# A megakernel on one core: the latents of seven batches move from a stage of their own into the attention stage that reads them

## The chip, the core and the metric

The kernel runs on 1 core of one Trainium2 chip as a single program. The metric is the device time in microseconds: the median of the runs. One execution was taken by the hardware profiler, and every row below is from that execution. Engines: PE is TensorE (PEld its weight loads), DVE is VectorE, ACT is ScalarE, POOL is GpSimd, SP is SyncE, which here only issues transfers.

## What is computed

Two layers on `x` of 8 batches x 512 tokens x 512 columns and a context of 8 batches x 77 tokens x 512. Layer 0 is a cross-attention and a routed slot block; layer 1 is a perceiver attention, whose queries, called latents here, come from the normalised token stream, and a choice of one expert out of 8 per token. The part around the change:

```python
# layer 0's last step, per batch (64 slots):   x2 = x1 + alpha @ vo + bo
x  = x + out                          # out = (alpha @ slot_values) @ wo + bo
# layer 1:
xn = layernorm(ctx_1024, ln_x_g, ln_x_b)            # 8 x 77 x 512
ln = layernorm(_layernorm(x), ln_l_g, ln_l_b)       # 8 x 512 x 512: the latents z
q  = ln @ Wq                                        # 16 heads of 64
k, v = split(concatenate((xn, ln), axis=1) @ Wkv)   # 77 + 512 keys
attn = softmax(where(mask, q k^T, -max))
out  = layernorm((attn @ v) @ Wout, ln_o_g, ln_o_b)
x    = x + out                                      # then the experts
```

All products are in float32: a tensor is kept as a high part in a rounded format and a low part (what the rounding left), and a product takes three matmuls (high x high, low x high, high x low; `product`, the records of L119 to L121).

## The kernel before, in words

The program runs in stages, one after the other, each a function with one instruction list per engine; all engines meet between stages. `build_slots` (L999) makes the slot values, `build_latents` (L1325) all latents and the context's keys and values, `build_perceiver` (L1661) the attention, `build_experts` (L2135) the rest. `two_layers` (L2836) calls them in this order.

**Latents stage.** SP loads the context rows at the start of the stage, and the token rows x1 of batch 2 and after into a ring of three buffers; x1 of batches 0 and 1 was loaded by the slots stage (L1099). For batch b, TensorE runs `read_out(b+1)` (four products alpha x vo with a row of ones for the bias, L1478), `transposed(b)` (16 transposes, L1486), `keys(b)` (24 matmuls of 308 columns for a pair of heads of all batches' context) and one or two `values` items (12 matmuls of 512 columns). VectorE runs `add_and_measure(b)` (adds the product to x1, L1608; statistics, L1611; aggregate, L1616), then the normalise (L1631), the low parts of the latents (L1641), of the keys (L1646) and of the values (L1651). GpSimd raises the variance to the power -1/2. ScalarE applies gain and bias (L1556), makes the high parts (L1560, L1574, L1582) and stores the latents' low part. The context's own path at the start: statistics (L1594), normalise (L1623), transposes (L1495, L1500), gain and bias (L1537), high (L1546) and low parts (L1638). Two banks serve keys and values; the value tile `Vst` is single, and ScalarE waits for its store (`V_out`) before it fills it for the next chunk (L1582, store L1423).

**Perceiver.** 128 heads of 4 ticks each; a tick n is 128 queries of one head against 589 keys, and each engine goes through the ticks in a loop written by hand, so the order of its work is fixed. TensorE in tick n issues the scores of tick n+1 (L1942, L1944), and, by n mod 8 (a pair of heads), transposes of the probabilities (L1955), the weighted sums (L1971, L1972) and the queries, keys and values of the next pair. The transposes, queries, keys and values share three banks `W`; `claim` takes the one released longest ago and waits for its readers. VectorE in tick n: reciprocal of the row sums (L2109), minimum over the scores (L2113), reads of the `W` banks (low parts `PTl`, keys `U`, values, all L2066), the addition of the output (L2098). ScalarE: exponential (L2034), high parts of the same banks (L2005), the copy and the high part of the output (L2053). GpSimd: probabilities times the reciprocal (L1880), and the output's low part (`low_part`, L1874), one per pair at tick 2 of a head. SP loads the latents of a batch (`load`, L1770), the keys, and stores the outputs (`store`). At the start GpSimd clears `Ql`, `Um` and the tails of `U`, 20 signals in all, and TensorE waits for all of them ahead of its first product:

```python
pe.wait_ge(setup, 20)
for n in range(1 - LEAD, STEPS + 2 * NT + 1):
    g, t = divmod(n, NT)
```

Of the kernel before, what the change touches and what calls it, by code (L numbers as in the profile page):

```python
# [20 lines left out]
P = 128  # L21
# [977 lines left out]
def build_slots(nc, orders, a, si_s, vo_s, Wq, Wkv, Wout_s, gh_s, WihT, x1_s):  # L999
# [11 lines left out]
    with ExitStack() as ctx:  # L1011
# [71 lines left out]
        def _(sp):  # L1083
# [15 lines left out]
            for n in range(2):  # L1099
                sp.dma_start(stage(n), x1_s[n:n + 1].rearrange("b (t p) d -> p (b t) d", p=P)).then_inc(x1_in, 16)  # L1100
# [5 lines left out]
            sp.wait_ge(x1_in, 32)  # L1106
# [218 lines left out]
def build_latents(nc, orders, a, x1_s, alphaT_s, vo_s, x2_s, z_s, Kc_s, Vc_s, Wkv, ahead):  # L1325
# [13 lines left out]
    RING = 3  # L1339

    with ExitStack() as ctx:
# [18 lines left out]
        rows_c = [f32(z_hi[1][:, k, :]) for k in range(KT - 1)] + [f32(z_lo[1][0:LAST, 0, :])]  # L1360
# [3 lines left out]
        setup, small, ones_row, cx_in = sem("setup"), sem("small"), sem("ones_row"), sem("cx_in")  # L1364
        x1_in = [sem(f"x1_in{r}") for r in range(RING)]
# [10 lines left out]
        batch = lambda b: 0 <= b < B  # L1376
        v_items = [(k, h) for k in range(KT) for h in range(2)]
        v_of = lambda b: v_items[b * len(v_items) // B:(b + 1) * len(v_items) // B]
        place = {"x2": lambda b, t: (b * NT + t) % 3, "zT": lambda b, c: 3 + (b * C + c) % 3, "cT": lambda c: 3 + c % 3,
# [20 lines left out]
        def _(sp):  # L1400
            flat = a["ctx_1024"].rearrange("b s d -> (b s) d")
            def load_small(b):
                m = b % 2
                if b >= 2:
                    sp.wait_ge(*pe_s.after("x2", b - 2, NT - 1))
# [3 lines left out]
            def load_x(b):  # L1409
                r = b % RING  # L1410
                if b >= RING:
                    sp.wait_ge(x2_out[r], 16 * (b // RING))
                    sp.wait_ge(*dve_s.after("xn", b - RING, NT - 1))
                sp.dma_start(X[r], x1_s[b:b + 1].rearrange("b (t p) d -> p (b t) d", p=P)).then_inc(x1_in[r], 16)
# [12 lines left out]
            for k in range(KT):  # L1427
                sp.dma_start(rows_c[k], flat[k * P:k * P + rows_of(k), :]).then_inc(cx_in, 16)
            for dst, src in smalls:
                sp.dma_start(dst, src).then_inc(small, 16)  # L1430
            load_small(1)
            load_x(2)
            for b in range(B):
                sp.wait_ge(*dve_s.after("free", "x2", b, NT - 1))
                sp.dma_start(x2_s[b:b + 1].rearrange("b (t p) d -> p (b t) d", p=P), X[b % RING]).then_inc(x2_out[b % RING], 16)
                if batch(b + 2):
                    load_small(b + 2)
                if batch(b - 1):
                    for q, h in [i for i in v_of(b - 1) if i[1]]:
                        values_out(q)  # L1440
                    keys_out(b - 1)
                if batch(b + 2) and b > 0:
                    load_x(b + 2)
            for q, h in [i for i in v_of(B - 1) if i[1]]:
                values_out(q)
            keys_out(B - 1)
            for r in range(RING):
                sp.wait_ge(x2_out[r], 16 * len(range(r, B, RING)))
# [5 lines left out]
        def _(pool):  # L1454
# [8 lines left out]
            for b in range(B):  # L1463
# [7 lines left out]
        def _(pe):  # L1471
# [52 lines left out]
            for b in range(B):  # L1524
                if batch(b + 1):
                    read_out(b + 1)
                transposed(b)
                keys(b)
                for k, h in v_of(b):
                    values(k, h)  # L1530

        @block.scalar
        def _(act):
# [14 lines left out]
            def latents(b):  # L1548
                m = b % 2
                if b >= 2:  # L1550
                    act.wait_ge(z_out[m], 32 * (b // 2))
                for c in range(C):
                    act.wait_ge(*pe_s.after("zT", b, c))
                    if b >= 2:
                        act.wait_ge(*dve_s.after("lo", b - 2, C - 1))
# [12 lines left out]
            for b in range(B):  # L1568
                latents(b)
# [6 lines left out]
                low_out(b)  # L1576
# [6 lines left out]
            for m in range(2):  # L1583
                act.wait_ge(z_out[m], 32 * (B // 2))

        @block.vector
        def _(dve):
# [3 lines left out]
            for k in range(KT):  # L1591
                r = rows_of(k)
                dve.wait_ge(cx_in, 16 * KT)
# [7 lines left out]
            def add_and_measure(b):  # L1601
                r, m = b % RING, b % 2
                dve.wait_ge(*dve_s.after("c var"))
                if b >= 2:
                    dve.wait_ge(x1_in[r], 16 * (b // RING + (r == 2)))
# [7 lines left out]
                if b >= 2:  # L1613
                    dve.wait_ge(*pool_s.after("ve", b - 2))
# [4 lines left out]
            add_and_measure(0)  # L1619
# [4 lines left out]
            for b in range(B):  # L1624
                r, m = b % RING, b % 2
                dve.wait_ge(*pool_s.after("rstd", b))
                dve.wait_ge(*dve_s.after("var", b))
                if b >= 1:
                    dve.wait_ge(*pe_s.after("zT", b - 1, C - 1))
# [3 lines left out]
                if batch(b + 1):  # L1633
                    add_and_measure(b + 1)
                if b == 0:
                    for c in range(C):
                        dve.wait_ge(*act_s.after("zc hi", c))
                        dve.tensor_tensor(zc[1][:, c, :], zc_full[c][:, :], f32(zc[0][:, c, :]), ALU.subtract).then_inc(*dve_s.mark("zc", c))  # L1638
                for c in range(C):
                    dve.wait_ge(*act_s.after("hi", b, c))  # L1640
                    dve.tensor_tensor(z_lo[m][:, c, :], full[m][:, c, :], f32(z_hi[m][:, c, :]), ALU.subtract).then_inc(*dve_s.mark("lo", b, c))  # L1641
# [19 lines left out]
def build_perceiver(nc, orders, a, z_s, Kc_s, Vc_s, o_s, xs_s, mask_s, Wq, Wkv, Wout_s):  # L1661
# [25 lines left out]
    with ExitStack() as ctx:  # L1687
# [315 lines left out]
        def _(act):  # L2003
# [26 lines left out]
            for n in range(1 - LEAD, STEPS + 2 * NT + 1):  # L2030
# [25 lines left out]
                if t == 3:  # L2056
                    probabilities(g - 1, 4)
# [848 lines left out]
```

## Time and profile before

| what | us |
|---|---|
| median of 3 runs (2,917.95 to 2,927.77) | 2,923.05 |
| the profiled execution | 2,921.61 |
| its span | 2,919.8 |
| latents stage, from the trace | 828.5 to 999.7 |

A row of a timeline reads: start, duration, engine, line and operation, output<-inputs, partitions x elements, and in brackets the idle time of the engine just before it with what ended it. A row with xN groups N instructions in a row. In the page's groups the columns are busy time, mean ns of one, idle before and its releaser. In the windows the columns are the stretch, its length, the busy time of PE, PEld, DVE, ACT and POOL, then PEclk, the mean clock granted to TensorE as a share of full speed, the busy share of the DMA engines and GB/s. In the waits: the waiting engine and line, whom it waited for, us in total, times, the longest.

### The profile page before, as it was taken

The numbers are of one execution on the slowest core, as the hardware profiler recorded it, in microseconds if no ns is written. First come the engines' busy times: TensorE is split into PE (matmuls) and PEld (weight loads), VectorE is DVE, ScalarE is ACT, GpSimd is POOL, SyncE is SP. The second block draws the span as 40 slices with busy tenths as digits, with TensorE's granted clock in tenths as the row PEclk, the third lists the DMA queues.
The fourth block names the chain that finished last, engine by engine and source line by source line (L and its number), as shares of the span: only waits on it lengthen the run. The fifth ranks groups of instructions, "written<-read, shape, count | busy, mean of one in ns | idle before, by whom it ended". The sixth has DMA issues, their size and how long they took to land. (4 is left out here: it accounts for less than half of the span.)

```text
span 2919.8 us, 41005 instructions
## 1 busy us (share of the span) xinstructions
PE 2646.1 (91%) x14566; PEld 2188.7 (75%) x14566; DVE 2023.6 (69%) x4005; ACT 1517.6 (52%) x2897; POOL 1522.0 (52%) x1149
## 2 busy tenths in 40 slices
PE   6699999986778699999999999999999998799698
PEld 5577777763436588888888888888888887677476
DVE  3677777742546377777777777777777777577666
ACT  2234334331213277777777777777777777111175
POOL 2355544320000166666666666666666666465555
PEclk9899999998878899999999999999999999899899
DMA  5212222133348633334333343233433314668475
GB/s 188 56 54 56 56 57 57 41 96 128 139 145 312 228 74 80 106 83 115 81 77 109 80 118 81 75 111 76 122 80 77 109 51 136 210 238 288 157 275 187
DMA packets 212526, 351.15 MB, mean 120 GB/s; under 512 B 75839, under 2 KB 82370, under 8 KB 204631
## 3 DMA queue, kind: packets, MB, share of 16 engines
q1 hardware_dynamic: 193539, 284.89, 32.8%
q0 software_dynamic: 11680, 45.02, 4.2%
q10 hardware_dynamic: 7104, 18.61, 1.6%
q8 instruction: 117, 1.92, 0.3%
q14 instruction: 86, 0.70, 0.1%
HBM read 172.47 MB, written 156.64 MB: 113 GB/s over the span
## 5 line engine op out<-in xcount | busy, mean ns | idle before, releaser
L1880 POOL TENSOR_SCALAR pa_Pr<-pa_Pr,pa_rs 128x590 f32<-128x590 f32 x512 | 902.4, 1769 | 485.1 <-DVE pa_rs L2109 484.9
L2113 DVE TENSOR_REDUCE pa_least<-pa_S 128x1 f32<-128x590 f32 x512 | 390.7, 763 | 230.0 <-PE pa_S L1944 227.9
L2034 ACT ACTIVATE pa_Pr<-pa_S,pa_least 128x590 f32<-128x590 f32 x512 | 385.5, 753 | 99.4 <-DVE pa_least L2113 96.0
L2066 DVE TENSOR_TENSOR pa_PTl<-pa_W,pa_PTh 128x512 fp32r<-128x512 f32 (+1 forms) x640 | 421.2, 684 | 20.5 <-ACT pa_PTh L2005 16.4
L2005 ACT ACTIVATE pa_PTh<-pa_W 128x512 fp32r<-128x512 f32 (+1 forms) x640 | 367.0, 596 | 58.4 <-PE pa_W L1955 47.1
L1955 PE MATMUL pa_W<-pa_ident,pa_Pr 128*128 128x128 f32 (+1 forms) x2560 | 369.7, 275 | 0.6
L1955 PEld LDWEIGHTS pa_W<-pa_ident,pa_Pr 128*128 128x128 f32 (+1 forms) x2560 | 302.4, 142 | 30.0 <-POOL pa_Pr L1880 2.8
L1971 PE MATMUL pa_O<-pa_PTh,pa_V 128*128 128x512 f32 (+1 forms) x640 | 289.2, 452 | 18.6 <-DVE pa_PTl L2066 14.4
L1972 PE MATMUL pa_O<-pa_PTl,pa_V 128*128 128x512 f32 (+1 forms) x640 | 253.4, 396 | 0.0
L1942 PE MATMUL pa_S<-pa_U,pa_Qh 128*128 128x296 f32 (+1 forms) x1024 | 228.9, 305 | 7.5 <-ACT pa_Pr L2034 0.5
L1942 PEld LDWEIGHTS pa_S<-pa_U,pa_Qh 128*128 128x128 f32 x1024 | 183.2, 188 | 55.5 <-ACT pa_Pr L2034 21.3
L1944 PE MATMUL pa_S<-pa_Um,pa_Ql 128*128 128x296 f32 (+1 forms) x1024 | 222.7, 299 | 0.0
L514 POOL TENSOR_TENSOR l_E<-l_E,l_rs 128x1232 f32<-128x1232 f32 x32 | 81.1, 2533 | 204.0 <-DVE l_rs L916 204.0
L1944 PEld LDWEIGHTS pa_S<-pa_Um,pa_Ql 128*128 128x128 f32 x1024 | 166.4, 189 | 0.0
L1971 PEld LDWEIGHTS pa_O<-pa_PTh,pa_V 128*128 128x128 f32 (+1 forms) x640 | 121.4, 190 | 45.0 <-DVE pa_PTl L2066 36.1
L119 PE MATMUL pa_W<-Wkv_hi,pa_z_hi 128*128 128x256 f32 x512 | 144.9, 283 | 0.0
L120 PE MATMUL pa_W<-Wkv_lo,pa_z_hi 128*128 128x256 f32 x512 | 144.2, 282 | 0.0
L121 PE MATMUL pa_W<-Wkv_hi,pa_z_lo 128*128 128x256 f32 x512 | 143.9, 281 | 0.0
L1972 PEld LDWEIGHTS pa_O<-pa_PTl,pa_V 128*128 128x128 f32 (+1 forms) x640 | 123.0, 192 | 5.2
L2560 ACT ACTIVATE ex_xT_hi<-ex_bank 128x512 fp32r<-128x512 f32 x92 | 53.4, 599 | 141.3 <-PE ex_bank L2456 134.9
L119 PE MATMUL pa_W<-pa_z_hi,Wq_hi 128*128 128x512 f32 x256 | 106.9, 418 | 17.8 <-POOL pa_Ql L1871 17.8
L2005 ACT ACTIVATE pa_U<-pa_W 64x512 fp32r<-64x512 f32 x128 | 75.8, 592 | 89.7 <-PE pa_W L121 88.1
(503 smaller groups left out, 6545.6 us busy)
## 6 DMA issues: line engine op xcount, KB each, us to landing
xs_s<-pa_Ql SPq DMA_DIRECT2D x57, 576.0 KB
pa_Um<-pa_U SPq DMA_DIRECT2D x128, 147.5 KB
pa_Qh<-pa_Qh SPq DMA_DIRECT2D x128, 128.0 KB
o_s<-pa_O_hi SPq DMA_DIRECT2D x64, 256.0 KB, 2.0
o_s<-pa_O_lo SPq DMA_DIRECT2D x64, 256.0 KB, 2.3
Wkv_hi<-o_s SPq DMA_DIRECT2D x8, 2048.0 KB, 11.3
Wkv_lo<-o_s SPq DMA_DIRECT2D x8, 2048.0 KB, 17.0
l_xa<-x SPq DMA_DIRECT2D x8, 1024.0 KB, 6.5
```

What stands on the lines that cost most here:

```text
L119: pe.matmul(out, a[0], b[0], start=first, stop=False)
L120: pe.matmul(out, a[0], b[1], start=False, stop=False)
L1880: pool.tensor_scalar(p, p, rs[:, g % 2, t:t + 1], None, ALU.mult).then_inc(*pool_s.mark("probs", n))
L1942: pe.matmul(out[:, a0:a1], qh, U[p % 2][x][:, a0:a1], start=True, stop=False)
L1944: m = pe.matmul(out[:, a0:a1], ql, Um[p % 2][x][:, a0:a1], start=False, stop=True)
L1955: m = pe.transpose(bank_of[u][0:KEYS[c], t * P:(t + 1) * P], Pr[g % 2][:, t, c * P:c * P + KEYS[c]], ident[:, :])
L1971: pe.matmul(Oc[:, :], v, PTh[0:n, r, :], start=(c == 0), stop=False)
L1972: pe.matmul(Oc[:, :], v, PTl[0:n, r, :], start=False, stop=(c == NC - 1)).then_inc(*pe_s.mark("PV", g, c))
L2005: act.activation(out, src, ACT.Copy, scale=scale).then_inc(*act_s.mark("hi", *name))
L2034: act.activation(Pr[g % 2][:, t, :], scored[n % 2], ACT.Exp, scale=-1.0, bias=least[:, g % 2, t:t + 1], accum_out=rs[:, g % 2, t:t + 1]).t ...
L2066: dve.tensor_tensor(out, src, f32(hi_ap), ALU.subtract).then_inc(*dve_s.mark(*name))
L2113: dve.tensor_reduce(least[:, g % 2, t:t + 1], scored[n % 2], AX, ALU.min).then_inc(*dve_s.mark("least", n))
```

## The change

Four things change together.

1. The latents stage keeps batch 0 only (`RING, FIRST = 1, 1`), and its order is turned: the context goes first, its rows now loaded by the slots stage in place of x1 of batch 1; then come keys and values for all eight pairs of heads, with batch 0's latents after the first round. Keys are stored ahead of values.
2. The latents of batches 1 to 7 are made in the perceiver as 28 tiles of 128 rows, one every 12 ticks (`APART`), each spread over ticks -2 to 8 from its beginning: fetch, row of ones, residual product, add and statistics, store of x2, power, normalise, transposes, gain and bias, high part, low part, and the stores of both. The two new TensorE steps claim `W` banks. SP's load of a batch waits for the stores of its latents.
3. To make room the output's low part overwrites its sum: ScalarE's copy of the next output waits for the store (`o_out`) instead of for the low part. The high part comes at tick 1 of a head, not at tick 2, and so does the low part.
4. At the start VectorE clears `Um` and the tails of `U` (8 signals, `blanks_done`), GpSimd only `Ql`; TensorE waits for both at its first scores instead of ahead of its first product.

The diff, cut to its core:

```diff
@@ build_slots, SP
-            for n in range(2):
-                sp.dma_start(stage(n), x1_s[n:n + 1].rearrange("b (t p) d -> p (b t) d", p=P)).then_inc(x1_in, 16)
+            sp.dma_start(stage(0), x1_s[0:1].rearrange("b (t p) d -> p (b t) d", p=P)).then_inc(x1_in, 16)
+            flat = a["ctx_1024"].rearrange("b s d -> (b s) d")
+            whole = flat.shape[0] // P
+            sp.dma_start(stage(1)[:, 0:whole, :], flat[0:whole * P, :].rearrange("(k p) d -> p k d", p=P)).then_inc(x1_in, 16)
+            sp.dma_start(stage(2)[0:flat.shape[0] - whole * P, 0, :], flat[whole * P:, :]).then_inc(x1_in, 16)
@@ build_latents
-    RING = 3
+    RING, FIRST = 1, 1
...
+            for b in range(PAIRS):
+                keys_out(b)
+                for q, h in [i for i in v_of(b) if i[1]]:
+                    values_out(q)
...
-            read_out(0)
-            context()
-            for b in range(B):
-                if batch(b + 1):
-                    read_out(b + 1)
-                transposed(b)
+            context()
...
+            for b in range(FIRST):
+                read_out(b)
+            for b in range(PAIRS):
                 keys(b)
                 for k, h in v_of(b):
                     values(k, h)
+                if batch(b):
+                    transposed(b)
@@ build_perceiver
+        APART = 3 * NT
+        tiles = [(b, t) for b in range(1, B) for t in range(NT)]
+        begins = {STEPS // B * (b - 1) + APART * t: i for i, (b, t) in enumerate(tiles)}
+        tile_at = lambda n, late: begins.get(n - late)
@@ SP
             def load(b):
+                if b:
+                    sp.wait_ge(z_out, 32 * NT * b)
...
+                if p == 0:
+                    sp.wait_ge(blanks_done, 8)
@@ GpSimd
-                    pool.memset(f32(Um[m][x][:, :]), 0.0).then_inc(setup, 1)
-            for m in range(2):
-                for x in range(2):
-                    pool.memset(f32(U[m][x][:, T + SK:Z]), 0.0).then_inc(setup, 1)
...
-                if t == 2 and g >= 3 and g % 2 == 1:
+                if t == 1 and g >= 3 and g % 2 == 1:
                     low_part((g - 3) // 2)
+                i = tile_at(n, 2)
+                if i is not None:
+                    pool.wait_ge(*dve_s.after("x2 var", i))
+                    pool.tensor_scalar(lve, lmv[:, 1:2], 1.0 + EPS, EPS * EPS, ALU.mult, ALU.add).then_inc(*pool_s.mark("x2 ve", i))
+                    pool.wait_ge(*pool_s.after("x2 ve", i))
+                    pool.tensor_tensor(lrstd, lve, minus_half, ALU.pow).then_inc(*pool_s.mark("x2 rstd", i))
@@ TensorE
             def scores(n):
...
+                if n == 0:
+                    pe.wait_ge(setup, 13)
+                    pe.wait_ge(blanks_done, 8)
...
-            pe.wait_ge(setup, 20)
+            def residual(i):
+                u = ("x2", i)
+                claim(u)
+                pe.wait_ge(x_in, 32 * (i + 1))
+                pe.wait_ge(vo_in, 16 * (i // NT + 2))
+                pe.wait_ge(*dve_s.after("ones", i))
+                pe.matmul(bank_of[u][:, :], alphas[0:NS + 1, :], vo[:, :], start=True, stop=True).then_inc(*pe_s.mark(*u))
+                release(u)
+            def latent(i):
+                u = ("zT", i)
+                claim(u)
+                pe.wait_ge(*dve_s.after("xn", i))
+                for c in range(C):
+                    m = pe.transpose(bank_of[u][:, c * P:(c + 1) * P], ln[:, c * P:(c + 1) * P], ident[:, :])
+                m.then_inc(*pe_s.mark(*u))
+                release(u)
...
+                if tile_at(n, 0) is not None:
+                    residual(tile_at(n, 0))
+                if tile_at(n, 4) is not None:
+                    latent(tile_at(n, 4))
@@ ScalarE: fetch at tick -2, x2 store at 2, high part at 6, its store at 7, the low part's store at 8
+                    act.wait_ge(x2_out, 16 * (i + 1))
+                    act.wait_ge(*dve_s.after("read", "zT", i))
+                    act.activation(l_hi, ln[:, :], ACT.Copy).then_inc(*act_s.mark("z hi", i))
...
-                        act.wait_ge(*pool_s.after("O lo", p - 1))
+                        act.wait_ge(o_out, 32 * p)
                     copy(O[x * HD:(x + 1) * HD, :], Oc[(1 - x) * HD:(2 - x) * HD, :], "low", g - 2)
@@ VectorE
-            dve.wait_ge(setup, 20)
+            for m in range(2):
+                for x in range(2):
+                    dve.memset(f32(Um[m][x][:, :]), 0.0).then_inc(blanks_done, 1)
+                    dve.memset(f32(U[m][x][:, T + SK:Z]), 0.0).then_inc(blanks_done, 1)
+            dve.wait_ge(setup, 13)
...
+            def add_and_measure(i):
+                dve.wait_ge(*pe_s.after("x2", i))
+                dve.tensor_tensor(lx[:, :], bank_of["x2", i][:, :], lx[:, :], ALU.add).then_inc(*dve_s.mark("read", "x2", i))
...
+            def scaled(i):
...
+                for c in range(C):
+                    m = dve.tensor_scalar(ln[:, c * P:(c + 1) * P], bank_of["zT", i][:, c * P:(c + 1) * P], gain[0][:, c:c + 1], gain[1][:, c:c + 1],
+                                          ALU.mult, ALU.add)
...
+            def latent_low(i):
+                dve.wait_ge(*act_s.after("z hi", i))
+                dve.tensor_tensor(ln[:, :], ln[:, :], lx[:, :], ALU.subtract).then_inc(*dve_s.mark("z lo", i))
...
+                for late, work in ((-1, ones), (1, add_and_measure), (3, normalised), (5, scaled), (7, latent_low)):
+                    if tile_at(n, late) is not None:
+                        work(tile_at(n, late))
```

## Rows read from the trace of the kernel before

**Rows 1.** Windows of three stretches: the latents stage, its rounds, the perceiver.

```profile
828.50:999.70 171.20, 124.57 (x524) 90.96 (x524) 100.09 (x207) 59.45 (x102) 14.05 (x22) 0.82 0.72 263
...
862.00:990.00 128.00, 106.69 (x472) 81.00 (x470) 78.75 (x160) 48.31 (x84) 9.38 (x13) 0.88 0.80 300
...
1100.00:2400.00 1300.00, 1282.70 (x7962) 1128.05 (x7961) 1006.24 (x1877) 942.43 (x1933) 873.43 (x513) 1.00 0.34 91
```

**Rows 2.** Waits of VectorE, weight loads and GpSimd in the perceiver, 1100 to 2400.

```profile
DVE pa_least L2113 <- PE pa_S L1944: 207.5, 177, 1.8
...
PEld pa_O L1971 <- DVE pa_PTl L2066: 24.9, 64, 1.2
...
POOL pa_Pr L1880 <- DVE pa_rs L2109: 429.4, 285, 3.1
```

**Rows 3.** Timeline of the latents stage, TensorE.

```profile
853.73 3.62 PE L1478 MATMUL la_bank<-la_vo,la_aT 65*128 65x512 f32 x8
...
861.60 0.41 PE L119 MATMUL la_bank<-la_zc_hi,Wkv_hi 128*128 128x308 f32 x1 [2.13 <-DVE la_zc_lo L1638]
...
894.55 0.39 PE L119 MATMUL la_bank<-la_zc_hi,Wkv_hi 128*128 128x308 f32 x1
...
899.62 0.50 PE L119 MATMUL la_bank<-Wkv_hi,la_zc_hi 128*128 128x512 f32 x1 [1.42 <-DVE la_K_lo L1646]
...
902.53 2.74 PE L1478 MATMUL la_bank<-la_vo,la_aT 65*128 65x512 f32 x6
```

**Rows 4.** Timeline of the latents stage, the context's path, VectorE and ScalarE.

```profile
836.86 2.47 DVE L1594 BATCH_NORM_STATS2 la_cstats<-la_z_hi 128x6 f32<-128x512 f32 x4 [7.11 <-DMA la_z_lo<-ctx]
...
848.42 1.88 DVE L1623 TENSOR_SCALAR la_z_hi<-la_z_hi,la_cmv,la_crstd 128x512 f32<-128x512 f32 x4
...
855.56 1.32 ACT L1546 ACTIVATE la_zc_hi<-la_K_hi 128x616 fp32r<-128x616 f32 x2
```

**Rows 5.** Timeline: a value store on SP's queue, and ScalarE's next fill.

```profile
919.91 0.34 SPq L1423 DMA_DIRECT2D Vc_s<-la_V  x1
...
923.91 0.60 ACT L1582 ACTIVATE la_V<-la_bank 128x512 fp32r<-128x512 f32 x1 [4.75 <-PE la_bank L1478]
```

**Rows 6.** Timeline of the change of stages, SP's queue and TensorE.

```profile
991.02 0.32 SPq L1423 DMA_DIRECT2D Vc_s<-la_V  x1
...
1000.38 0.42 SPq L1770 DMA_DIRECT2D pa_z_lo<-z_s  x1
...
1007.42 0.79 PE L119 MATMUL pa_W<-pa_z_hi,Wq_hi 128*128 128x512 f32 x1 [17.79 <-POOL pa_Ql L1871]
```

**Rows 7.** DMA issues, 985 to 1020: KB each, median us to landing.

```profile
pa_z_lo<-z_s SPq DMA_DIRECT2D x1, 1024.0 KB, 6.9
```

**Rows 8.** Timeline of a pair of heads in the perceiver, VectorE and TensorE.

```profile
1783.54 0.77 DVE L2113 TENSOR_REDUCE pa_least<-pa_S 128x1 f32<-128x590 f32 x1 [1.75 <-PE pa_S L1944]
...
1787.39 1.28 DVE L2066 TENSOR_TENSOR pa_PTl<-pa_W,pa_PTh 128x512 fp32r<-128x512 f32 x2
...
1788.13 0.66 PE L1955 MATMUL pa_W<-pa_ident,pa_Pr 128*128 128x128 f32 x4
1788.54 0.48 PE L1971 MATMUL pa_O<-pa_PTh,pa_V 128*128 128x512 f32 x1
```

**Rows 9.** Groups of the latents stage, VectorE: busy us, mean ns | idle before.

```profile
L1608 DVE TENSOR_TENSOR WihT<-la_bank,WihT 128x512 f32<-128x512 f32 x32 | 20.9, 687 | 7.4 <-PE la_bank L1478 7.3
L1641 DVE TENSOR_TENSOR la_z_lo<-la_z_lo,la_z_hi 128x512 fp32r<-128x512 f32 x32 | 20.0, 686 | 9.2 <-ACT la_z_hi L1560 9.2
...
L1631 DVE TENSOR_SCALAR la_xn<-WihT,la_mv,la_rstd 128x512 f32<-128x512 f32 x32 | 15.3, 542 | 0.0
```

**Rows 10.** The page's part 5, GpSimd's product of the probabilities.

```profile
L1880 POOL TENSOR_SCALAR pa_Pr<-pa_Pr,pa_rs 128x590 f32<-128x590 f32 x512 | 902.4, 1769 | 485.1 <-DVE pa_rs L2109 484.9
```

**Rows 11.** Timeline of the experts' start, GpSimd and VectorE.

```profile
2505.98 5.47 POOL L2338 TENSOR_TENSOR ex_R<-ex_R,ex_b_bc 128x512 f32<-128x512 f32 x4 [12.62 <-DMA ex_b_bc<-L_xattn_ln_o_b]
...
2507.24 1.81 DVE L2760 TENSOR_TENSOR ex_h_lo<-ex_LT,ex_h_hi 8x512 fp32r<-8x512 f32 x1
```

More of the change, by code:

```diff
@@ L1462, in _ @@
             pool.tensor_tensor(crstd[:, :], cve[:, :], minus_half[:, :], ALU.pow).then_inc(*pool_s.mark("c rstd"))
-            for b in range(B):
+            for b in range(FIRST):
                 m = b % 2
@@ L1566, in low_out @@
                 act.dma_start(z_s[1][b], f32(z_lo[b % 2][:, :, :])).then_inc(z_out[b % 2], 16)
-            for b in range(B):
-                latents(b)
+            for b in range(PAIRS):
                 for h in range(2):
@@ L1582, in _ @@
                     act.activation(hi, src, ACT.Copy).then_inc(*act_s.mark("hi", "V", k, h))
-            for m in range(2):
-                act.wait_ge(z_out[m], 32 * (B // 2))
+                if batch(b):
+                    latents(b)
+                if batch(b - 1):
+                    low_out(b - 1)
+            act.wait_ge(z_out[0], 32)
         @block.vector
@@ L1632, in _, with low @@
                                       ALU.subtract, ALU.mult).then_inc(*dve_s.mark("xn", b, t))
[L1633 to L1638, printed above, removed]
+            def low(b):
+                m = b % 2
                 for c in range(C):
@@ L1641, in _ @@
                     dve.tensor_tensor(z_lo[m][:, c, :], full[m][:, c, :], f32(z_hi[m][:, c, :]), ALU.subtract).then_inc(*dve_s.mark("lo", b, c))
+            add_and_measure(0)
+            normalised(0)
+            for b in range(PAIRS):
                 for h in range(2):
@@ L1651, in _ @@
                     dve.tensor_tensor(lo, src, f32(hi), ALU.subtract).then_inc(*dve_s.mark("free", "V", k, h))
+                if batch(b):
+                    low(b)
 def read_out_tiles(Wq, Wkv, T):
@@ L1851, in _ @@
             sp.wait_ge(o_ahead, 32 * AHEAD)
+            sp.wait_ge(x2_out, 16 * len(tiles))
             for m in range(2):
@@ L2057, in _ @@
                     probabilities(g - 1, 4)
+                if tile_at(n, -2) is not None:
+                    fetch(tile_at(n, -2))
+                if tile_at(n, 2) is not None:
+                    keep(tile_at(n, 2))
+                i = tile_at(n, 6)
+                if i is not None:
+                    act.wait_ge(x2_out, 16 * (i + 1))
+                    act.wait_ge(*dve_s.after("read", "zT", i))
+                    act.activation(l_hi, ln[:, :], ACT.Copy).then_inc(*act_s.mark("z hi", i))
+                i = tile_at(n, 7)
+                if i is not None:
+                    act.wait_ge(*act_s.after("z hi", i))
+                    latent_out(0, i)
+                i = tile_at(n, 8)
+                if i is not None:
+                    act.wait_ge(*dve_s.after("z lo", i))
+                    latent_out(1, i)
                 if STEPS <= n < STEPS + 4:
```

141 lines of the change are left out of this document (79 added, 62 removed).

## The prediction, made before the changed kernel was built

> **What bounds the kernel now.** I read the stages first. The stretch of windows [rows 1] shows that the latents stage lasts 171.2 us (828.5 to 999.7) with TensorE busy for 124.57 of them, at a granted clock of 0.82 of full speed, while in 1,300 us of the perceiver TensorE is busy for 1,282.70 (98.7%) at 1.00, VectorE for 1,006.24 (77%) and GpSimd for 873.43 (67%). So the latents stage has 47 us in which TensorE does nothing, and the perceiver has 17 in 1,300. Then the waits of the perceiver [rows 2]: VectorE idles 207.5 us before its minimum over the scores, for want of scores, so it runs ahead of TensorE and catches up there; GpSimd idles 429.4 us; the weight loads of the weighted sums wait 24.9 us for VectorE's low part of the transposed probabilities (`PTl`). TensorE is the bound of the perceiver, and VectorE is the engine that first holds it up. Last I read the latents timeline [rows 3, 4], the store waits [rows 5] and the change of stages [rows 6, 7].
>
> About 0.3% (8.8 us) is what a measurement of this kernel can tell from no change. The sum goes against the profiled execution, 2,921.6 us, which is 1.4 below the median.
>
> **Latents stage: what goes.** Three terms.
>
> First key product: now at 861.60. The context's statistics begin at 836.86 after 7.11 us of waiting for the context's load [rows 4]; with the rows loaded in the slots stage that goes: 7.1. Its normalise starts 11.6 us later, at 848.42, because the adds and statistics of batch 0 sit between; for what it really needs (five statistics and five aggregates, then GpSimd's power) I estimate 5.3 us from the 2.47 of the first four [rows 4], so 6.3 go. At the end, the low parts of the context wait behind the statistics of batch 1: high parts begin at 855.56 [rows 4], the first product follows at 861.60, 2.13 us of that a shown wait for the low part; I take 4.2. Sum 17.6: first key product near 844.
>
> Rounds: they last 128 us (861.60 to about 989.6). What remains is eight times keys and ten value items. Keys take 3.6 us (894.55 to 898.2, which is 899.62 less the wait of 1.42), a value item 2.9 (899.62 to 902.53) [rows 3]: 28.8 + 29 = 57.8. To this come bank waits like that of 1.42: keys and values share two banks, and I count eight, 11. The single buffer of the values is stored in 4.0 us (issued at 919.91, the next copy at 923.91 after 4.75 of waiting [rows 5]); four such waits, mostly behind keys, 6. Batch 0's own latents between: 2.2 us of transposes and about 6 in which VectorE's adds and normalise delay the keys' low part, 8. Sum 83, so 45 go.
>
> Tail: the last value store at 991.02 is now followed by the key stores, and the next stage's first `z` load goes out at 1000.38 [rows 6], 9.4 us later. With keys stored first only the 4.0 us of the value store and the change of stage are left; 4 go.
>
> Total 17.6 + 45 + 4 = 67. Bounds: 52, if each of the four store waits lies open for its 4.0 (10 more) and batch 0 costs 5 more; 72 without most of batch 0's delay.
>
> **Perceiver start.** TensorE no longer waits for the cleared buffers but for `z` alone. Its first product starts at 1007.42, after 17.79 us of idling put down to GpSimd's last fill [rows 6]. The low half of `z`, issued at 1000.38, lands 6.9 us later [rows 7]: 1007.3. So what gives way is a wait that another ends at the same time: 0.1 us, and VectorE's own clearing (four fills, before its mask row) lies under the load. Cost 0; bounds 2 gained, 1 lost.
>
> **Perceiver: what comes.** 28 tiles. TensorE: the residual product (two records a tile; eight records, four tiles, took 3.62 us [rows 3]) 0.9, four transposes 0.41 (1788.13 to the next product at 1788.54 [rows 8]); 1.31 x 28 = 36.7 us, all on the path, since TensorE is the bound.
>
> VectorE: add 0.69, statistics of the same 512 columns, aggregate, normalise 0.54, four scalings of 128 columns, low part 0.69 [rows 9], with the row of ones about 4.4 us a tile, 123 us in all, against 294 idle in the 1,300 of [rows 1]. In sum it fits; in order it does not always. VectorE's queue is fixed, and a tile's work is behind one tick's minimum and ahead of the next tick's reads. What is late next: the first `PTl` of a head is read from 1787.39, two reads in 1.28, so the first ends near 1788.03, and TensorE's next transposes start at 1788.13 [rows 8]. There is no slack there. Ahead of it, VectorE idled 1.75 us at 1783.54.
>
> The tiles begin every 12 ticks, so 14 begin at tick 0 of a pair's eight and 14 at tick 4. In the first kind add, statistics and aggregate (1.5 us) fall in tick 1, where the residual's own TensorE time and VectorE's idling cover them; the four scalings fall in tick 5, ahead of that first read, and cost about 0.4 net. Per tile 1.31 + 0.4 = 1.7. In the second kind add and statistics fall in tick 5: 1.5 at that read; normalise waits for GpSimd's power, which now sits behind two probability products of 1.77 us [rows 10] and the output's low part: 0.8; the query products need a bank that the scalings release: 1.0; less 0.8 that stalled there before. Per tile 1.31 + 2.5 = 3.8. Sum 14 x 5.5 = 78 us (41 of it waits). Bounds: 37 (no wait) and 103 (each tile 0.9 more).
>
> Taken at nothing, with their cover: ScalarE's high part and DMA issues (ScalarE does not hold up TensorE in [rows 2]); the batch load on SP, which now waits for the last latents store, issued some ticks before its queries, with the output stores and key loads queued behind; the output copy's wait for the output store instead of GpSimd, whose low part now comes a tick earlier; that earlier part itself, GpSimd having 429.4 us idle. If a cover goes, I take what a late `PTl` costs now, 24.9 us over the stretch [rows 2], as the price; the upper bound has room for it.
>
> **Sum.** 2,921.6 - 67 + 78 = 2,932.6, and with 1.4 to the median **2,934 us**. A tile costs 2.78 us against a break-even of 67 / 28 = 2.39.
>
> **A rule on the shared port.** The trace shows VectorE operations with two SBUF inputs being held up: the 8x512 low part took 1.81 us while GpSimd ran its four two-input adds of 5.47 us from 2505.98 [rows 11]; a low part of as many columns takes 0.69 in the latents stage [rows 9], where GpSimd is nearly idle. The new low part has two SBUF inputs, and GpSimd is busy two thirds of the perceiver. But in every such row GpSimd reads two tensors, and the probabilities' product reads one. The Trainium skill (SBUF — State Buffer, section "SBUF: two separate sides") says that a VectorE operation with two SBUF inputs and a GpSimd operation that reads SBUF exclude each other for a whole instruction; by that, one-input products block too, and the sum would be some 17 us higher. No row shows that; the sum goes by the rows, and the case is rival (b).
>
> **Rivals.**
> (a) *Faster: the waits vanish in VectorE's idling.* The 207.5 us before the minimum are slack ahead of each tick; each product that TensorE is given is also time for VectorE. If the tile's work is absorbed, only TensorE's 36.7 is paid: 2,921.6 - 67 + 37 + 1.4 = 2,893. It decides where waits fall under 67/28 - 1.31 = 1.08 us a tile. For: VectorE at 77%. Against: no slack at 1788.13.
> (b) *Slower still: the low part waits for GpSimd's product.* GpSimd runs 67% of the time, a random arrival waits half of 1.77: 0.6 us, 28 times 17 us, 50 at most: 2,951 to 2,984. VectorE would show low parts of over 1 us. Against: no row with one input.
> (c) *The latents stage gives back less.* TensorE, now idle for a larger share of it, works at the lower clock (it was 0.88 in the rounds [rows 1]) and waits for each value store: 52 instead of 67, 2,949.
> (d) *The start gate does nothing.* That is already in the sum at 0; it moves no number.
>
> **How the numbers follow.** The forecast 0.45, (a) 0.32, (b) 0.13, (c) 0.10. Faster by over 0.3% (below 2,914): nearly all of (a), 0.30, and the lowest part of the forecast, 0.05: 0.35. Within (2,914 to 2,932): 0.02 of (a), 0.17 of the forecast and 0.01 of (c): 0.20. Slower: 0.45. The forecast's own range is 2,910 to 2,958. The range for 8 in 10 takes in (a) down to 2,886 (a saving of 72 and the start's 2) and (b) and (c) up to 2,960.
>
> **What would show it.** Right: first key product near 844, perceiver start at 930 to 934, its first product 7 us behind that; TensorE's busy time in the perceiver up by 37; a pair of heads some 4 us longer where a tile begins at its fourth tick, with transposes and weighted sums waiting for `PTl`; normalise waiting for GpSimd. Wrong: VectorE's idling before the minimum down by about 120 us with no new TensorE wait (a); low parts over 1 us (b); perceiver start after 945 (c). If the latents stage ends before 925, the first sum was too small; if batch loads appear on TensorE's waits, the store chain was not hidden.

## The result, and the profile after

The changed kernel takes 2,966.97 us (median of 4 runs, 2,962.85 to 2,970.97) against 2,923.64: a ratio of 1.0149, 95% interval 1.0125 to 1.0174. It is slower by 43 us; the forecast was slower, 2,934, with a range that ended at 2,960. The profiled executions differ by as much: 2,963.73 against 2,921.61, spans 2,961.9 against 2,919.8, 42.1 us.

First the windows, with the columns of [rows 1]: the latents stage, and 1,400 us of the perceiver.

```profile
825.95:932.25 106.30, 73.01 (x356) 59.92 (x356) 33.57 (x67) 24.44 (x46) 3.24 (x8) 0.87 0.34 128
1032.00:2432.00 1400.00, 1343.03 (x8221) 1160.25 (x8220) 1113.88 (x2160) 972.97 (x1986) 900.84 (x569) 1.00 0.40 106
```

The latents stage went from 171.2 to 106.3 us. In the perceiver TensorE's busy share fell from 98.7% to 95.9%: it now has 57 us of idling in 1,400, and it had 17 in 1,300. The waits of that stretch, of TensorE and of VectorE:

```profile
PE pa_W L119 <- DVE pa_xn_next L2202: 24.7, 26, 1.0
PE pa_O L1975 <- DVE pa_PTl L2135: 14.5, 20, 1.0
PE pa_W L1959 <- DVE pa_PTl L2135: 7.6, 13, 0.6
...
DVE pa_least L2218 <- PE pa_S L1948: 162.3, 134, 1.8
...
DVE pa_xn_next L2196 <- POOL pa_norm L1883: 20.5, 13, 1.6
```

The first row is a product that waits for a bank which the four scalings (L2202) have not yet read, about once per tile; the next two are the late `PTl` of [rows 2]; the last is normalise waiting for GpSimd, in 13 tiles. VectorE still idles 162 us ahead of its minimum (207.5 in a window 100 us shorter before): most of the slack was not used.

From the first minimum over the scores to the last, in the kernel before and in the changed one, TensorE's busy time rose by 50 us, where the forecast had 37, and its idle time from 21 to 80 us (busy times are partly modelled, so some waiting may stand in the first figure):

```profile
1019.54:2466.99 1447.45, 1426.63 (x8850) 1253.93 (x8849) 1122.27 (x2096) 1051.21 (x2157) 975.33 (x572) 1.00 0.34 93
```

```profile
954.00:2510.79 1556.79, 1476.46 (x9019) 1274.81 (x9018) 1224.22 (x2374) 1070.03 (x2187) 996.89 (x629) 0.99 0.40 106
```

One tile of the second kind, on TensorE's and VectorE's timelines:

```profile
1195.00 0.66 PE L1959 MATMUL pa_W<-pa_ident,pa_Pr 128*128 128x128 f32 x4 [0.58 <-DVE pa_PTl L2135]
...
1199.50 0.55 DVE L2196 TENSOR_SCALAR pa_xn_next<-pa_x_next,pa_norm 128x512 f32<-128x512 f32 x1 [1.58 <-POOL pa_norm L1883]
...
1205.05 0.50 PE L119 MATMUL pa_W<-pa_z_hi,Wq_hi 128*128 128x512 f32 x1 [1.02 <-DVE pa_xn_next L2202]
```

It shows the three steps in their order: the transposes of the probabilities late by 0.58 us for `PTl`, which stands behind the addition and its statistics in VectorE's queue, normalise behind GpSimd, the queries behind the scalings.

To place the time I took the starts of the minimum over the scores (VectorE, L2113 before, L2218 after; 512 of each, one per tick) and compared the two kernels from tick to tick. With the starts of the stages this gives the whole difference:

| stretch | before | after | difference |
|---|---|---|---|
| start to the latents stage | 828.55 | 825.95 | -2.6 |
| latents stage | 171.2 | 106.3 | -64.9 |
| perceiver's start to its first minimum | 19.8 | 21.7 | +1.9 |
| first minimum to the last | 1,447.4 | 1,556.8 | +109.3 |
| last minimum to the end | 452.8 | 451.1 | -1.7 |

The first row is not the change's: the stages before it are the same, and in the runs below that start lies between 827 and 834. The 109.3 us fall into three parts. A half pair of heads is four ticks; the one before the last takes 15.2 us more. The first pair takes 7.9 more, where later pairs with a tile at the same place take some 2.4 (3.7 in two): 5.5 of it are put down to the start. The remaining 88.6 us are what is left for the 28 tiles, 3.2 each.

The last pair, on SP's and ScalarE's timelines and TensorE's:

```profile
2475.80 0.53 SPq L1781 DMA_DIRECT2D Wq_lo<-Wout_s  x1
2476.38 0.70 SPq L1784 DMA_DIRECT2D Wkv_hi<-o_s  x1
2477.12 3.94 SPq L1784 DMA_DIRECT2D Wkv_lo<-o_s  x1
2481.11 7.05 SPq L1776 DMA_DIRECT2D o_s<-pa_O_hi  x1
2488.20 0.52 SPq L1776 DMA_DIRECT2D o_s<-pa_O_sum  x1
...
2498.16 0.59 ACT L2030 ACTIVATE pa_O_sum<-pa_O 64x512 f32<-64x512 f32 x1 [14.79 <-DMA o_s<-pa_O_sum]
...
2499.68 0.86 PE L1946 MATMUL pa_S<-pa_U,pa_Qh 128*128 128x296 f32 x2 [14.30 <-ACT pa_Pr L2085]
```

SP loads the next stage's data early (three transfers of 2 MB), and the store of an output stands behind them on the same queue; the issue alone of its two halves takes until 2488.7. ScalarE's copy of the next output (L2030) waits 14.79 us for that store, everything in ScalarE's queue stands, and TensorE waits 14.30. Before, the copy waited for GpSimd's low part, and the store was waited for later, by the high part, for about 3 us. On ScalarE's timeline of the kernel before:

```profile
2469.70 0.63 ACT L2053 ACTIVATE pa_O_hi<-pa_O_sum 128x512 fp32r<-128x512 f32 x1 [3.02 <-DMA o_s<-pa_O_lo]
```

The first pair, TensorE's timeline and its windows:

```profile
940.66 0.80 PE L119 MATMUL pa_W<-pa_z_hi,Wq_hi 128*128 128x512 f32 x1 [16.05 <-DMA pa_z_lo<-z_s]
...
959.15 1.10 PE L1984 MATMUL pa_W<-pa_vo,pa_xn_next 65*128 65x512 f32 x2 [3.23 <-DMA pa_vo<-vo_s]
```

```profile
956.00:959.20 3.20, 0.05 (x1) 0.09 (x1) 1.43 (x3) 1.78 (x5) 1.79 (x1) 1.00 0.36 101
959.20:963.50 4.30, 4.30 (x12) 3.31 (x13) 2.28 (x5) 0.83 (x2) 1.43 (x1) 0.61 0.00 0
```

The first product indeed waits for `z` alone now, and starts 8.4 us into the stage where it was 7.7 [rows 6]. The first residual product then waits 3.23 us for the slot values' fetch, and the next 4.3 us run at a granted clock of 0.61, most of them at 1.2 GHz instead of 2.4. By an estimate from the second window that loses another 1.7 us (0.39 of 4.3), so the idle time is paid about one and a half times.

### The profile page after: what moved, and what is told of

The parts are those of the page before. It is cut to its first block and busy times, and to the rows that moved or that the text cites. A ratio compares the mean times of both kernels' runs of the same rounds, so it can differ in the third digit from the quotient of the medians.

```text
span 2961.9 us, 41403 instructions
## 1 busy us (share of the span) xinstructions
PE 2640.8 (89%) x14566; PEld 2175.1 (73%) x14566; DVE 2063.4 (70%) x4153; ACT 1500.4 (51%) x2869; POOL 1528.8 (52%) x1184
## 5 line engine op out<-in xcount | busy, mean ns | idle before, releaser
L2218 DVE TENSOR_REDUCE pa_least<-pa_S 128x1 f32<-128x590 f32 x512 | 389.5, 761 | 180.2 <-PE pa_S L1948 176.9
L2030 ACT ACTIVATE pa_PTh<-pa_W 128x512 fp32r<-128x512 f32 (+1 forms) x640 | 368.3, 595 | 88.3 <-PE pa_W L1959 78.5
L1946 PE MATMUL pa_S<-pa_U,pa_Qh 128*128 128x296 f32 (+1 forms) x1024 | 242.3, 318 | 18.2 <-ACT pa_Pr L2085 14.5
L2214 DVE RECIPROCAL pa_rs<-pa_rs 128x1 f32<-128x1 f32 x512 | 80.9, 158 | 64.5 <-ACT pa_Pr L2085 61.9
## 6 DMA issues: line engine op xcount, KB each, us to landing
Wkv_hi<-o_s SPq DMA_DIRECT2D x8, 2048.0 KB, 11.4
```

Source lines behind the costliest of these rows:

```text
L1946: pe.matmul(out[:, a0:a1], qh, U[p % 2][x][:, a0:a1], start=True, stop=False)
L2030: act.activation(out, src, ACT.Copy, scale=scale).then_inc(*act_s.mark("hi", *name))
L2218: dve.tensor_reduce(least[:, g % 2, t:t + 1], scored[n % 2], AX, ALU.min).then_inc(*dve_s.mark("least", n))
```

## The experiments

Two theories of the 28 tiles. *Place*: what a tile costs is set by the tick into which VectorE's steps fall, so most of it can be saved by moving them. *Load*: TensorE and VectorE have that much more to do, and a tile costs some 3.1 us wherever it stands. All runs build on the changed kernel, except where the kernel before is named. Costs per tile are read as above, from the starts of the minimum every four ticks, less the kernel before; a sum of several numbers is a tile's successive half pairs.

**e1: the stores first.**

```diff
-                if p == PAIRS - 1:
-                    ahead()
                 if p >= 2:
                     store(p - 2)
+                if p == PAIRS - 1:
+                    ahead()
```

> In the last pair of heads SP stores the outputs of the pair before last ahead of the 2 MB of early loads for the next stage, not behind them. Theory (the new wait of ScalarE's output copy for the output store is what costs 14.8 us there): the copy's wait for the store falls under 2 us, the last eight ticks lose about 14 us, the time falls by 12 to 15. Rival (the 15 us are the transfers themselves, which only fill the queues): the wait moves to the next store or to the next stage's wait for the early loads, and the time falls by less than 5.

Measured: 2,953.7 us, a ratio to the kernel before of 1.0106 (1.0081 to 1.0131), 13.3 less than the change. The half pair that took 15.16 us more than before takes 0.23 more. On ScalarE's timeline:

```profile
2490.36 0.59 ACT L2030 ACTIVATE pa_O_sum<-pa_O 64x512 f32<-64x512 f32 x1 [0.82 <-DMA o_s<-pa_O_sum]
```

And on SP's:

```profile
2486.89 0.33 SPq L1776 DMA_DIRECT2D o_s<-pa_O_hi  x1
```

The wait of 14.79 us is 0.82, the store's issue 0.33, and nothing behind it became longer (449.9 us from the last minimum to the end, 451.1 in the change). The wait was the cost, not the transfers: all three early loads (6 MB, of which the expectation names 2) are still made, behind the store.

**e2: all tiles at the first tick.**

```diff
-        begins = {STEPS // B * (b - 1) + APART * t: i for i, (b, t) in enumerate(tiles)}
+        starts = lambda b: (0, 12, 24, 40) if b == 1 else (-8, 8, 24, 40)
+        begins = {STEPS // B * (b - 1) + starts(b)[t]: i for i, (b, t) in enumerate(tiles)}
```

> All tiles but one begin at the first of a pair's eight ticks instead of half of them at the fifth (begins 0, 12, 24, 40 for batch 1 and -8, 8, 24, 40 after it); no instruction is added or left out. Theory (a tile's price is set by which VectorE tick its work falls into): 13 tiles go from about 3.7 us to about 2.3, the perceiver gets shorter by 16 to 20 us. Rival (28 tiles cost some 3.1 us each wherever they stand, since VectorE and TensorE have that much more to do): change within 4 us.

Measured: 2,977.05 us, 1.0181 (1.0158 to 1.0204): longer, a miss for both theories. By half pairs it splits. A tile at the first tick inside a batch costs 0.87 + 1.35 - 0.50 + 0.47 = 2.2 us in most places (1.2 to 1.9 more in four); in the change a tile at the fifth costs 3.02 + 1.14 - 0.14 = 4.0, or 3.02 + 1.15 - 0.59 = 3.6. So place matters. But at each change of batch one half pair now takes 4.4 to 7.0 us more than before. TensorE's waits and, at one such place, its windows:

```profile
PE pa_W L1985 <- DMA pa_vo<-vo_s: 11.4, 6, 3.5
```

```profile
1126.00:1132.50 6.50, 4.74 (x26) 3.58 (x26) 5.21 (x13) 4.22 (x10) 5.93 (x4) 1.00 1.00 388
1132.50:1138.50 6.00, 4.25 (x17) 2.94 (x15) 3.31 (x7) 1.68 (x4) 2.11 (x3) 0.72 0.59 179
```

The first tile of a batch now begins while the next batch's latents are loaded: the transfer engines are busy all the time (1.00, 388 GB/s), its fetch comes late, and in the 6 us around the wait the granted clock is 0.72.

**e7: e2 with that fetch six ticks ahead.**

```diff
+        fetches = {n - (6 if t == 0 and b > 1 else 2): i for n, i in begins.items() for b, t in [tiles[i]]}
...
-                if tile_at(n, -2) is not None:
-                    fetch(tile_at(n, -2))
+                if n in fetches:
+                    fetch(fetches[n])
```

> The kernel of e2 with the first fetch of each batch six ticks ahead of its tile instead of two, so that it is issued before the 2 MB load of the next batch's latents and not behind it. Theory (e2 paid 3.5 to 6 us at each change of batch because the first residual product waits for a fetch that shares the queues with that load): the half pair that took 4.4 to 7.0 us more than before takes 0.9 to 1.5, the perceiver is 18 to 28 us shorter than in e2. Rival (there the queries wait for the latents themselves, since the last tile now ends four ticks later): the excess stays, or moves into the queries' wait.

Measured (one run): 2,951.37 us. The perceiver is 25.4 us shorter than in e2 (1,541.9 from first to last minimum, 1,567.3 there), the wait for the fetch is gone from TensorE's waits, and the half pair takes 1.6 to 2.2 more than before, a little above the expected 0.9 to 1.5. Against the change (1,556.8) the perceiver is 14.9 us shorter with the same instructions, only moved.

**e3: the first batch's tiles four ticks later.**

```diff
+        starts = lambda b: (4, 16, 28, 40) if b == 1 else (0, 12, 24, 36)
```

> The four tiles of batch 1 begin four ticks later (4, 16, 28, 40), so that the first fetch is not waited for at the start of the perceiver; the other batches stay. Theory (the first pair is 5.5 us longer than other pairs with a tile because TensorE waits 3.2 us for the first slot values and then works at the lower clock): the first pair loses 5 to 7 us, and the time falls by about 5, since the first of the four tiles then falls on a fifth tick (1.4 dearer). Rival (the first pair is long because its own queries and keys come late there): change under 2 us.

Measured (one run): 2,966.52 us. The first 64 ticks take 13.2 us more than before instead of 18.0, 4.8 less; the first pair alone loses 4.4, a little under the 5 to 7 expected. The total doesn't show it and by itself would read for the rival, because elsewhere half pairs differ by as much (the perceiver is 1.3 us shorter in all), and one run can't tell 5 us.

**e4: the tiles at the seventh tick.**

```diff
+        starts = lambda b: (0, 13, 26, 39) if b == 1 else (-10, 6, 22, 38)
...
-(5, scaled), (7, latent_low))
+(5, scaled), (9, latent_low))
...
-                i = tile_at(n, 8)
+                i = tile_at(n, 10)
```

> The tiles begin at the seventh tick of a pair (-10, 6, 22, 38; batch 1: 0, 13, 26, 39), with the low part and its store two ticks later, so that normalise, scalings and low part fall on ticks 1, 3 and 7, where VectorE idles ahead of the next minimum, and the four transposes' bank is next claimed two products later. Theory (place sets the price): 24 tiles cost 1.4 to 2.0 us each instead of 3.1, the perceiver gets shorter by 25 to 40 us. Rival (load sets it): within 5 us. A third outcome, longer than the kernel it is made from: add and statistics, 1.6 us of VectorE at tick 7, delay the next pair's first scores and cost more than the rest gives.

Measured (one run): 2,969.73 us; the perceiver is 12.9 us longer than the change's (1,569.7), outside both theories' ranges. A tile costs 2.15 + 0.68 + 0.27 - 0.45 = 2.65, less than the change's mean of 3.2 and more than the 1.4 to 2.0 of the theory; at the change of batch the late fetch of e2 comes back (18.7 us of waits over six tiles, 5.5 to 6.7 us more per half pair). And a new wait came, 30.0 us in 42 places, of the scores for the exponential. The perceiver is longer, as in the third outcome, but not for its reason: what stands ahead of those exponentials is ScalarE's own part of a tile. TensorE's timeline and ScalarE's at one place of each kind:

```profile
1199.26 0.54 PE L1947 MATMUL pa_S<-pa_U,pa_Qh 128*128 128x296 f32 x2 [0.65 <-ACT pa_Pr L2086]
...
1222.36 0.54 PE L1947 MATMUL pa_S<-pa_U,pa_Qh 128*128 128x296 f32 x2 [0.60 <-ACT pa_Pr L2086]
```

```profile
1197.84 0.63 ACT L2119 ACTIVATE pa_x_next<-pa_xn_next 128x512 fp32r<-128x512 f32 x1
1198.38 0.73 ACT L2086 ACTIVATE pa_Pr<-pa_S,pa_least 128x590 f32<-128x590 f32 x1
...
1220.73 0.68 ACTq L2064 DMA_DIRECT2D pa_xn_next<-alphaT_s  x1
1221.46 0.75 ACT L2086 ACTIVATE pa_Pr<-pa_S,pa_least 128x590 f32<-128x590 f32 x1 [0.51 <-DVE pa_U L2136]
```

In 18 places it is the high part of the latents (11.6 us), in 24 the issues of the next tile's fetch (18.4 us). The prediction took both at nothing; in the change they fall elsewhere, and there this wait doesn't show.

**e5: the eighth tick.** With e1's stores, e4's later low part, and the fetch four or five ticks ahead (two in batch 1).

```diff
+        starts = lambda b: (0, 13, 26, 39) if b == 1 else (-9, 7, 23, 39)
...
+        fetches = {n - (5 if t == 0 and b > 1 else 4 if b > 1 else 2): i for n, i in begins.items() for b, t in [tiles[i]]}
```

> The stores of the last pair first, as in e1, and the tiles of batches 2 to 7 at the eighth tick of a pair (-9, 7, 23, 39; batch 1: 0, 13, 26, 39), with their fetch four or five ticks ahead instead of two, and the low part two ticks later. Add and statistics then fall on tick 0, normalise on 2, scalings on 4, low part on 0: the ticks after which VectorE idles (0.6, 1.2, 1.8, 0.6 us in the kernel before). Theory (place sets the price): 24 tiles cost 1.4 to 1.9 us each, hardly more than TensorE's own 1.3, no extra wait at the change of batch, and the time is 2,905 to 2,920, at or under the kernel before. Rival (load sets it, 3.1 a tile wherever): 2,950 to 2,957, as e1.

Measured: 2,949.42 us, 1.0091 (1.0062 to 1.0119). The change of batch is clean (2.2 us for its tile), but a tile costs 1.69 + 1.49 - 0.08 = 3.1: what the rival said. VectorE's waits show why:

```profile
DVE pa_least L2220 <- PE pa_S L1950: 108.1, 104, 1.8
DVE pa_xn_next L2204 <- PE pa_W L1994: 55.2, 25, 2.2
...
DVE pa_x_next L2187 <- PE pa_W L1986: 26.7, 19, 1.4
```

I had put VectorE's work on the right ticks and TensorE's on the wrong end of them. VectorE's tick n begins as soon as the scores of tick n are there, and TensorE issues those at the start of its own tick n-1: VectorE is a tick ahead. A product that TensorE issues at the end of its tick, behind the keys or values, is there only when VectorE's idle time is over; VectorE stood up to 2.2 us in front of the scalings, and was late with its reads of the banks that TensorE's transposes of the probabilities claim next. TensorE's waits:

```profile
PE pa_W L1961 <- DVE pa_U L2137: 25.6, 25, 1.3
PE pa_W L1961 <- DVE pa_V L2137: 11.0, 19, 0.6
```

**e8: e5 with TensorE's two steps ahead of the queries, keys and values of their tick**, and the very first fetch six ticks ahead.

```diff
+                if tile_at(n, 0) is not None:
+                    residual(tile_at(n, 0))
+                if tile_at(n, 4) is not None:
+                    latent(tile_at(n, 4))
                 if q_of(n) is not None:
                     query(q_of(n))
```

> The kernel of e5 with TensorE's two steps of a tile issued ahead of the keys and values of their tick instead of behind them, and the very first fetch four ticks earlier. In e5 a tile still cost 3.1 us (1.7 and 1.5 in the half pairs after its start and after its transposes): VectorE reached the scalings and the addition before TensorE had made their inputs (55 us and 27 us of waiting) and stood there, ahead of the next minimum. Theory (VectorE works one tick ahead of TensorE's loop, so a tile's product at the end of a tick comes too late for the idle time after it): both waits fall under 10 us, a tile costs 1.4 to 2.0, the first half pair loses 3 to 6, the time is 2,905 to 2,925. Rival (the price is TensorE's and VectorE's added work, and placing only moves it): a tile stays near 3.1, the time at 2,944 to 2,950.

Measured: 2,914.57 us (12 runs, 2,905.3 to 2,923.52), a ratio to the kernel before of 0.9971, 95% interval 0.9955 to 0.9986. It beats both kernels, the change by 52 us and the kernel before (2,922.4 beside it) by 8. VectorE's waits over 1032 to 2392, then TensorE's:

```profile
DVE pa_least L2220 <- PE pa_S L1950: 144.3, 147, 1.8
...
DVE pa_xn_next L2198 <- POOL pa_norm L1885: 24.1, 25, 1.0
...
PE pa_O L1977 <- DVE pa_PTl L2137: 6.9, 7, 1.0
PE pa_W L1961 <- DVE pa_Ql L2152: 2.7, 6, 0.6
```

Both of VectorE's waits of e5 are gone, and so are the 36.6 us that TensorE's transposes waited there; the perceiver is 38.4 us shorter than in e5. The 6.9 us of the weighted sums stood in the kernel before as well, and a tile costs 1.11 + 0.57 - 0.07 = 1.6 us, of which 1.3 are TensorE's own by the forecast's count. Normalise still waits for GpSimd in nearly every tile and costs nothing that shows, since it stands where VectorE idles. The first half pair takes 1.97 us more than before, in e5 5.62. From the first minimum to the last it takes 52.7 us more than before, where the change takes 109.3 more.

**e6: the start gate alone, in the kernel before.** VectorE clears `Um` and the tails of `U`; TensorE waits at its first scores.

```diff
-            pe.wait_ge(setup, 20)
...
+                if n == 0:
+                    pe.wait_ge(setup, 12)
+                    pe.wait_ge(blanks_done, 8)
```

> The kernel before with the fourth part of the change alone: VectorE clears half of the buffers, TensorE waits for them at its first scores. Theory (the first product waits for the latents' low half, which lands when the last fill ends): first product still 7 to 8.5 us after the stage's start, no change beyond 2 us. Rival (the gate was the limit): the first product 3 us or more earlier, the time 3 us or more lower.

Measured: 2,923.8 us (10 runs), 0.9993 (0.9977 to 1.0008): no difference. TensorE's timeline:

```profile
1009.27 0.80 PE L119 MATMUL pa_W<-pa_z_hi,Wq_hi 128*128 128x512 f32 x1 [17.61 <-DMA pa_z_lo<-z_s]
```

It starts 7.6 us into the stage (at 1001.68 there), 7.7 before [rows 6]: the load was the second wait behind the gate.

## Why the prediction was wrong

**Right.** The latents stage: 67 us predicted, 64.9 measured. First key product 15.2 us into the stage (841.18 less 825.95) where it was 33.1: 17.8 against 17.6. The rounds from there to the last product at about 924.6 take 83.4, against the 83 of the sum; here two errors cancel, which is luck. TensorE is busy for 65.0 us of them, where the products and transposes of the sum make 60, and waits 18.4, where the sum had 23 (11 for banks, 6 for the values' store, 6 for batch 0). One wait of 6.52 us, behind batch 0's adds and normalise on VectorE, is most of the 11.4 for the keys' low part; the values' low part has 7.0. The window, and that wait on TensorE's timeline:

```profile
841.18:924.60 83.42, 64.97 (x329) 54.83 (x328) 25.17 (x48) 17.82 (x35) 1.21 (x2) 0.92 0.38 149
```

```profile
852.22 0.79 PE L119 MATMUL la_bank<-Wkv_hi,la_zc_hi 128*128 128x512 f32 x1 [6.52 <-DVE la_K_lo L1621]
```

The tail is 7.6 instead of 10.1: 2.5 against 4. The start gate at 0: e6 says 0 in the kernel before, and in the changed one the start became 1.9 us longer, a little beyond the bound of 1. The direction, and the place of the tiles' waits: the late `PTl` (0.6 at the transposes and about as much at the weighted sums, where I had 1.5), the normalise behind GpSimd (1.6 of waiting), the queries' bank (1.0), all there in the second kind of tile, 3.6 to 4.0 us for a forecast 3.8. The total of that kind came out closer than its terms, which is in part luck.

**Wrong: the term "taken at nothing, with their cover".** In it stood "the output copy's wait for the output store instead of GpSimd". The prediction has no row for that store. From 1032 to 2432 it is nearly early enough: the copy waits for it 7.3 us, in five places. At the last pair the same queue carries 6 MB for the next stage ahead of the store, and the copy waits 14.8 us; e1 takes 13.3 us off the time by exchanging two calls. The kernel before had the same loads ahead of the same store and showed the sign, the 3.02 us above. The prediction did name a price for a lost cover, 24.9 us, with room in the upper bound; but that bound holds only the 25 us by which the tiles alone might be dearer. With this term at 15 the sum would have been 2,949, inside the range: it took the start and the tiles as well to leave it.

**Wrong: the start at 0.** The start was priced by the gate and by `z` alone. The first tile's fetch was left out: the first pair is 5.5 us longer for it, 3.2 of waiting and most of the rest at the lower clock behind it. Moving the tile (e3) gave back 4.8 us, and the earlier fetch of e8 3.7 in the first half pair against e5.

**Mis-sized: the tiles.** 88.6 us against 78 (14 x 5.5 is 77; the slip of 1 changes nothing). The second kind was right; the first kind costs 2.1 to 2.7 in most places (3.6 in two) where I had 1.7, because its scalings also hold up a bank (the 26 waits of 1.0 us are of both kinds, the queries' and the values').

**The rivals.** (a), waits absorbed, did not happen in this kernel; e8 shows that most of them can be: 1.6 us a tile, close to the 1.31 of its price, with nothing left out. The break-even of 2.39 holds: the change's 3.2 lies above it, e8's 1.6 below. What decided, from e5 to e8, was neither VectorE's total idling nor its tick alone, but whether TensorE's part is issued early enough in the tick for VectorE to do its part while it would idle. (b) fell: the new low part takes 0.680 to 0.684 us in all 28 tiles, 13 of them while GpSimd works on a product (below). (c) fell: the stage saved 64.9. Of (d), see e6.

**The sum, corrected** from the profiled execution: 2,921.6 - 2.6 - 64.9 + 1.9 + 5.5 + 88.6 + 15.2 - 1.7 = 2,963.6, which it took (the 88.6 being what the other terms leave). Against the forecast's 2,932.6 that is 15.2 for the store, 7.4 for the start, 10.6 for the tiles and 2.1 for the latents stage, less 4.3 before the stage and behind the last minimum.

Open: why the batches differ by up to 2 us (11.7 to 13.7 more per 64 ticks in the change, the first batch apart), which no run separates; and what the four tiles of batch 1 in e8 (14.9 us, where other batches take 6.5) would cost at better ticks, which was not tried.

## What to carry to other kernels

A step that is moved under another engine's work is priced by places, not by totals: the tick in which the busy engine idles, the point in the other engine's tick at which its input is issued, the queue behind which its transfer stands, and what an engine off the path then puts ahead of the others' work (ScalarE in e4); the same 28 tiles cost between 1.6 and 4.0 us each. When a wait is replaced by a later one of the same chain (store instead of compute), follow the queue that issues it through its worst moment, here the last pair, and not through the period. And a short stall of TensorE is not paid once: look at the granted clock right behind it.

## What the runs showed of the hardware that I had not expected

The contention of [rows 11] appears here only with two tensors on both sides. In e8 the new low part (VectorE, two SBUF inputs, L2210) lies wholly inside one of GpSimd's one-input products (L1877) in 19 of 28 tiles. Its line first (duration in ns: minimum, median, maximum), then on both timelines one such place, and the one tile that met GpSimd's two-input low part (L1871):

```profile
L2210 DVE TENSOR_TENSOR pa_xn_next<-pa_xn_next,pa_x_next x28: 673/678/1734, 986.7 to 2244.2; 128x512 f32<-128x512 f32 x28
```

```profile
1199.80 5.39 POOL L1877 TENSOR_SCALAR pa_Pr<-pa_Pr,pa_rs 128x590 f32<-128x590 f32 x3
...
1202.57 0.68 DVE L2210 TENSOR_TENSOR pa_xn_next<-pa_xn_next,pa_x_next 128x512 f32<-128x512 f32 x1
...
1028.73 1.28 POOL L1871 TENSOR_TENSOR pa_O_sum<-pa_O_sum,pa_O_hi 128x512 f32<-128x512 f32 x1
...
1028.81 1.73 DVE L2210 TENSOR_TENSOR pa_xn_next<-pa_xn_next,pa_x_next 128x512 f32<-128x512 f32 x1
```

Beside the one-input product it takes 0.68 us, as alone, and the product its 1.77; started 0.09 us behind the two-input operation it takes 1.73, 0.54 beyond that one's end. The Trainium skill (SBUF — State Buffer, section "SBUF: two separate sides") has a VectorE operation with two SBUF inputs excluded by any GpSimd operation that reads SBUF; the measurement decides here, and of GpSimd's operations beside this low part only the one with two tensors held it up (one place each in e8, e5 and e4, 1.73 to 1.75 us). Two tensors alone are not enough: in the kernel before, nine of the latents' low parts (L1641, two SBUF inputs) begin during GpSimd's power (L1468, two tensors of 128x4) and take 0.68 to 0.69 us.

A stall of 3.2 us of TensorE was followed by 4.3 us at a granted clock of 0.61, in a stretch that stood at 1.00 before and after; a stall of 1.75 us in e2 stands in 6 us at 0.72. And here a queue that had taken three transfers of 2 MB held its engine: SP's issue of a 256 KB store took 7.05 us behind them, and 0.33 when it went first in e1.
